# One Trainium2 core, a fused four-layer model: Mamba's front with dt's bias as a matmul row and the residual added by TensorE

## What is computed

```python
def mamba_block(x, Wi, cw, cb, Wx, Wdt, bdt, Alog, Dp, Wo):
    xz = x @ Wi.T
    xs, z = jnp.split(xz, 2, axis=-1)
    u = silu(causal_conv(xs, cw) + cb)
    xdbl = u @ Wx.T
    dt, Bc, Cc = jnp.split(xdbl, [8, 8 + 16], axis=-1)
    dt = jax.nn.softplus(dt @ Wdt.T + bdt)
    A = -jnp.exp(Alog)
    # h = exp(dt A) h + dt B u ;  y = C h
    y = scan(...) + u * Dp
    y = y * jax.nn.silu(z)
    return y @ Wo.T
for i in range(4):
    x = mamba_block(layer_norm(x, ln_w[i], ln_b[i]), ...) + x
```

## Time and profile before

| | us |
|---|---|
| median of 3 runs | 1874.89 (1874.24 to 1879.85) |
| the profiled execution, its own time | 1869.66 |
| its span, first to last instruction | 1867.8 |
| first scan-group instruction to last (L1049) | 110.3 to 1641.6 |
| mean granted TensorE clock over the span | 0.876 of full speed |

### The profile page before, as it was taken

How to read it: one execution, slowest core, us unless ns; L and a number is a source line. 1 busy time by engine, 2 the same in 40 slices (tenths; PEclk the granted TensorE clock), 3 DMA queues, 4 the chain that set the end, 5 groups by cost and what they waited for, 6 DMA issues and landing times.

```text
span 1867.8 us, 28242 instructions
## 1 busy us (share of the span) xinstructions
PE 1482.4 (79%) x9417; PEld 1056.2 (57%) x9417; DVE 1481.1 (79%) x2326; ACT 1339.2 (72%) x2730; POOL 1325.9 (71%) x1767
## 2 busy tenths in 40 slices
PE   6677766666899988567878999778889986889975
PEld 2443433334677666434455777556667664667854
DVE  6588898899999899978987978887988998721254
ACT  4476656666998787767687878788887886654453
POOL 3158678777788789887766867799978897830046
PEclk7676776787999999787788999989999998989997
DMA  5033222433544334220334444332545433212300
GB/s 192 1 75 73 63 66 69 109 82 96 134 119 116 120 108 108 69 59 23 91 102 108 130 126 138 86 107 56 132 137 132 132 96 69 66 43 74 124 6 6
DMA packets 84591, 170.15 MB, mean 91 GB/s; under 512 B 9440, under 2 KB 14944, under 8 KB 84064
## 3 DMA queue, kind: packets, MB, share of 16 engines
q1 hardware_dynamic: 84448, 168.37, 32.9%
HBM read 99.12 MB, written 2.10 MB: 54 GB/s over the span
## 4 chain that ended last, share of the span: by engine, by line
PE 23%; DVE 14%; ACT 9%; POOL 7%; issue 3%; DMA 2%; SPq 0%; DVEq 0%; POOLq 0%; ACTq 0%
DVE m L1049 5%; DVE dtuB L1041 3%; POOL m L1060 3%; PE ps L1467 3%; ACT m L1025 3%; PE ps L1475 2%; PE ps L1314 2%; PE ps L1758 2%; PE ps L1182 2%; PE ps L1080 2%; PE ps L964 2%; POOL o L1660 1%; PE ps L1325 1%; POOL o L1655 1%; ACT L347 1%
## 5 line engine op out<-in xcount | busy, mean ns | idle before, releaser
L1060 POOL TENSOR_TENSOR m<-m 128x256 f32<-128x256 f32 x1024 | 906.7, 920 | 92.5 <-DVE m L1049 84.9
L1049 DVE TENSOR_TENSOR_SCAN m<-m,dtuB 128x1024 f32<-128x1024 f32 x256 | 584.4, 2283 | 32.8 <-PE ps L1080 9.6
L1025 ACT ACTIVATE m<-m,Aneg 128x255 f32<-128x255 f32 x1024 | 429.8, 497 | 24.3 <-DMA m<-m 17.0
L1041 DVE TENSOR_TENSOR dtuB<-m 128x1024 f32<-128x1024 f32 x256 | 347.5, 1357 | 14.0 <-DMA m<-spread 5.2
L1467 PE MATMUL ps<-o 128*128 128x256 f32 x512 | 149.0, 402 | 18.9 <-DVE X L1411 7.1
L1080 PE MATMUL ps<-m,w_const 128*32 128x256 f32 x2048 | 151.5, 426 | 10.2 <-POOL m L1060 10.2
L1434 ACT ACTIVATE o<-ps,w_mo 128x256 f32<-128x256 f32 x256 | 113.4, 470 | 60.1 <-PE ps L1467 58.6
L364 POOL TENSOR_TENSOR o<-o,mhalf 128x2 f32<-128x2 f32 x64 | 19.4, 304 | 170.2 <-DVE o L358 170.2
L1182 PE MATMUL ps<-o 128*128 128x256 f32 x512 | 125.8, 395 | 13.2 <-ACT o L1151 8.2
L964 PE MATMUL ps<-m,wc 128*128 128x256 f32 x512 | 134.4, 421 | 2.0 <-ACT m L385 2.0
L1475 PE MATMUL ps<-o 128*128 128x128 f32 x1024 | 128.8, 279 | 5.5 <-ACT o L1434 4.8
(11 more groups left out here) (251 smaller groups left out, 2909.7 us busy)
## 6 DMA issues: line engine op xcount, KB each, us to landing
m<-m SPq DMA_DIRECT2D x256, 256.0 KB, 4.8
m<-spread SPq DMA_DIRECT2D x64, 512.0 KB, 5.4
o<-in_mox SPq DMA_DIRECT2D x128, 256.0 KB, 3.1
o<-in_l1x SPq DMA_DIRECT2D x88, 256.0 KB, 3.1
w_mb<-in_mb SPq DMA_DIRECT2D x1, 2288.0 KB, 11.8
m<-in_cwr SPq DMA_DIRECT2D x1, 2048.0 KB, 15.6
w_l3f<-in_l3f SPq DMA_DIRECT2D x1, 1536.0 KB, 17.6
X<-in_x SPq DMA_DIRECT2D x4, 256.0 KB, 6.6
```

The lines of the kernel that those rows point to most:

```text
L1025: op = e.activation(dA[at % NA][:, j, 1:CH], R[q][:, h * CH + 1:h * CH + CH], ACT.Exp, scale=Aneg[:, l, 4 * g + j:4 * g + j + 1])
L1041: e.tensor_tensor(dtuB[:, :, :], bc(R[q][:, (2 + h) * CH:(3 + h) * CH].unsqueeze(1), 4, CH), Br[k % 2], ALU.mult).then_inc(S.dve, n.tick(f ...
L1049: e.tensor_tensor_scan(flat(G[at % NG]), flat(dA[at % NA]), flat(dtuB[:, :, :]), 0.0, ALU.mult, ALU.add).then_inc(S.dve, n.tick(f"s{g}"))
L1060: op = e.tensor_tensor(part, part, Cr[k % 2][:, j:j + 1, :], ALU.mult)
```

## The change

It does five things in the front, and the table of turns is new.

1. The bias of dt becomes a 41st row. W_x gets a zero column (41 outputs), the activation that copies them adds a per-partition value that is 1 in row 40 and 0 elsewhere, and W_dt gets the bias as its row 40. The constant "bdt" (2 columns) goes, "one" (1 column) comes.
2. The two Identity activations with the bias go. Abs reads the bank straight away; Ln writes the tile dtu instead of the bank; VectorE's last step reads dt from the bank and the logarithm from dtu.
3. TensorE adds the residual: before the wait for y, two matmuls of the identity with hs open the accumulation in the bank, and the output projection adds to them. VectorE's add is gone.
4. The norm's statistics and the normalization read the bank for l over 0. TensorE's first transpose then waits for both halves, since it overwrites the bank. For the last block X is added from the bank.
5. ScalarE copies the bank into hs for l over 0, after the statistics, in a turn of its own ahead of the normalization.

Turns of ORDER: on TensorE f goes from 192 to 224, on VectorE from 136 to 112, on ScalarE from 200 to 224; all other totals, and all of SyncE (577) and GpSimd (594), are as before. The a and b turns that stand ahead of a given s turn differ by -13 to +15 on TensorE (of 1056), -10 to +5 on VectorE (of 600), -7 to +7 on ScalarE (of 960), -6 to +2 on GpSimd and -4 to +3 on SyncE. After the last s turn, 182, 104, 174, 54 and 58 of them are left, in both tables.

```diff
-MB, NMB = cols([("win", 512), ("wx", 2, 40), ("wdt", 256), ("wout", 2, 128),
-                ("cb", 2), ("bdt", 2), ("alog", 8, 4), ("dp", 2), ("lnw", 1), ("lnb", 1)])
+MB, NMB = cols([("win", 512), ("wx", 2, 41), ("wdt", 256), ("wout", 2, 128),
+                ("cb", 2), ("one", 1), ("alog", 8, 4), ("dp", 2), ("lnw", 1), ("lnb", 1)])
...
 class Front, dve:
                     e.wait_ge(F.pe, n.pe("wo"))
-                    e.tensor_tensor(v.hs, ps2(b), v.hs, ALU.add).then_inc(F.dve, n.tick("hs"))
-                    e.wait_ge(F.dve, n.dve("hs"))
                     if l == NL - 1:
-                        e.tensor_tensor(X2(c), X2(c), v.hs, ALU.add).then_inc(F.dve, n.tick("X"))
+                        e.tensor_tensor(X2(c), X2(c), ps2(b), ALU.add).then_inc(F.dve, n.tick("X"))
                         if k < NU:
                             e.wait_ge(F.dve, n.dve("X"))
-                    yield
+                        yield
...
-                yield from norm_dve(e, n, F, v, v.hs)
+                yield from norm_dve(e, n, F, v, ps2(b) if l else v.hs)
                 e.wait_ge(F.act, n.act("ln"))
-                e.scalar_tensor_tensor(v.dt, v.dt, 0.0, halves_of(b), ALU.max, ALU.add).then_inc(F.dve, n.tick("dt"))
+                e.scalar_tensor_tensor(v.dt, halves_of(b), 0.0, v.dtu, ALU.max, ALU.add).then_inc(F.dve, n.tick("dt"))
...
 class Front, act:
-                norm_act(e, n, F, v, v.hs, v.xn)
+                if l:
+                    e.wait_ge(F.dve, n.dve("mv1"))
+                    e.copy(v.hs, ps2(b)).then_inc(F.act, n.tick("hs"))
+                    yield
+                norm_act(e, n, F, v, ps2(b) if l else v.hs, v.xn)
...
-                e.copy(v.xd[0:40, :], b[0:40, 0:CH]).then_inc(F.act, n.tick("xd"))
+                e.activation(v.xd[0:41, :], b[0:41, 0:CH], ACT.Identity, bias=m("one", l)[0:41, 0:1]).then_inc(F.act, n.tick("xd"))
                 yield
                 e.wait_ge(F.pe, n.pe("wd"))
-                for h in range(2):
-                    e.activation(v.dt[:, h, :], b[:, h * CH:h * CH + CH], ACT.Identity,
-                                 bias=m("bdt", l)[:, h:h + 1]).then_inc(F.act, n.tick(f"v{h}"))
-                e.wait_ge(F.act, n.act("v1"))
-                e.activation(v.dtu, v.dt, ACT.Abs).then_inc(F.act, n.tick("ab"))
+                e.activation(v.dtu, halves_of(b), ACT.Abs).then_inc(F.act, n.tick("ab"))
...
-                e.activation(halves_of(b), v.dtu, ACT.Ln, bias=1.0).then_inc(F.act, n.tick("ln"))
+                e.activation(v.dtu, v.dtu, ACT.Ln, bias=1.0).then_inc(F.act, n.tick("ln"))
...
 class Front, pe:
                     c, l = UNITS[k - 2]
+                    for i in range(2):
+                        e.matmul(b[:, cut(i)], ident, v.hs[:, i, :], start=i == 0, stop=False, skip_group_check=True)
+                    yield
                     e.wait_ge(F.dve, n.dve("y"))
                     for i in range(2):
                         for h in range(2):
-                            op = e.matmul(b[:, cut(i)], v.dtu[:, h, cut(i)], m("wout", l)[:, h, :], start=h == 0, stop=h == 1)
+                            op = e.matmul(b[:, cut(i)], v.dtu[:, h, cut(i)], m("wout", l)[:, h, :], start=False, stop=h == 1,
+                                          skip_group_check=True)
...
+                if l:
+                    e.wait_ge(F.act, n.act("xn1"))
                 turn_pe(e, n, F, b, v.xn)
```

More of the change, by code:

```diff
@@ L209 @@
     "sp":
[L210 to L213, removed]
+        "uf2s4fs4f2sfs7f3s8f3s8f3s8f3s8f3s8f3s8f2sa2s3afs4a6fa2sb3fs4fs3bfb2f2s4b2s4b3a3f3sasas6a3faf2s4a2s2a2b2sa2saf3sb"
@@ new lines @@
+        "a8ua3ua3ba2ba7b2ab2ab7ab2ab2ab5a3bab2a2f2b2abf3abab2aba2ba2ba3sf2afafbfsb7aba4sb2afa2fbsafbfsaf4sabfabf2b2abf3b2"
+        "s2a4b2abasf2a6saba2fbfa2fbf2a2sa3b2asaf2asa2fbfsfa2f2bsbfba2sf2b2f5sb10sb2afb4fs2f2bf2bsf2ab2sbf2saf3a2sf2a2b2a2"
+        "bafafab2afbaf2abasfsa2b3asfbasafa2fabfafabfaba2sbaba5fasbafbababfabfasfbafsfaba4b2a3bfa2b2saba2fba2ba2fbfbsb2fsf"
+        "bfa2b2a2babafabasba3fasa3fba2bfa4bafa2fabfbsb4ab4fab4sb3safa2b2abafb2fsafab2f2b3sb2f2b3sb2fa2bfb3fb3fa5bfsbafa4b"
+        "sbafab5afa2sa3fafbfbfsa4b2ababa4ba5sb2fafb2sba2b2f3af2sb6fb3sb4fba2babasb2f2ba2bafbfasafab2fa3safb2asbfaf3afasb4"
@@ new lines @@
+        "a4b3sf2aba2fbfafa2fbafba2sasba2babafbasa2fb2afbfasafa2fba2bfa3bsba2ba3b2fa2ba3b2abasa3b2abafbab2a2bfa2bafbsbafa2"
+        "fba2bsfab2ab2a3b2ab2sab2fbfb2abfb2fbsb3fbabafab2fb2a2b2abfab2sb2ab2ab7sfa2ba3f2bsf2afa3bab2a2safb2ababa3safa3b2a2"
+        "fsb2fbabfabfa3sfa3b2a3fba2b2asafba2b2afbafsbaf3asb2ab2asaba2f2b3afba2fas2afabafafba2sb2f2basa3fb2fabafa2b2f2bsb3"
+        "fb3ababsa2fba3bfa2fababasfbfbfbsb2ababfa3b6sb2fb2a2b4fsfab2fbsfb2fb2ab5ab5asfb2fb2safabfa3fa2f2bfasa3ba2bab4sa2b"
+        "fa6b2fa2sababa2b2sba5b2ab2aba2safa3baba2b2aba2ba3babababab2ababa6b2a2b2aba2b2aba2b3a2b3ab3a2ba2bababa4ba2ba2baba"
@@ new lines @@
+        "b2abab3ab2ab3ab2ab2abab2ab5ab8ab9a2ba3ba2b5a2b2a4b3ab3abab2a2bab2",
+    "dve":
+        "au2a7u2bu2b7a11ba2fb2fb3a7b5fb2sfs2fs2bsbsbsbsbs2b2s2fs10fafs7a2s2fa3fsfs4as5a2sa2fs2a2sbs2b2asa2fa2ba2fbsbs7bs3"
+        "b3sbfs8fs2fs3as5a2sb2fafa2b2sb3fbsbs8asfs11fsfs9a2f2afasfs3bsfs11b2fa2fbfbsbfs2fabasabab2sbs6fb2s7a2bfsfs2a2sabs"
+        "bas2bs3fs9fsfsas2a2sb2s3as2afsb3abs3fsafs3as8fsabs3fab2fs2asbs3as4ba2fs2abas2abs2afas3fsbsas5bs3a4fabfa2fsas2bs4"
+        "asbsasasb2s2a3ba3ba2fbasb2asa2s3asas2fs2af2a5fab6sb3s2bs2bsfbs4b8abs2fba2b2f2a2fab2s3bsbsb2absb2s4fs3a3fasfs2asa"
+        "s7basasasasfb2sbsbs2fbfs4bs5b4afsab2s5a2bfasfabsb2s7fs7asfa2fs4babsas3bfab2s2bas3as3fsas3fs2as2bs2b2abs2fbas2a2s"
+        "bfsa2fbasa2sbs4bs3faba2sa5bas3bas2ab2afsf2sfb2a6sa2basbsabas2afs2a2s2b3sasasa2bsb2s2fb2f2bs2bfbs2ba2s3b5saba2sba"
+        "b2s2fb2sbs3b2sfsfs2bs2asbs2bs2ba2fs5as2fsfs2as2b2s3as4fafb3fs3bs4as6fs4as2fbfsasb2s3bs4basfs2bs3basfsfsbs5bs5bfa2"
+        "sba2sbs2afsfsa2b2s3bsbsa2sa6fabs2b2a3s4a6ba2babs2afb2a2sbfa2b3s3aba2b2as5b5sb4asbab2s2aba2fafb5a4b2abab3a2bab2ab"
+        "ab3aba2b2a2baba2b5a3b2a6b3a2b3ab3a2ba2b2a5b8aba2b3ab",
@@ new lines @@
+    "act":
+        "a3ua4ua2ua2bua2ba2ba5b2ab3ab4ab2a2b6a3bafabf2abfb2faf2abab2as2bafabsabas2f2sasaf3bfb3sb2sba2sa2sba3s2bf2afbs2bsf4"
+        "as2af2sbafs2b2faf2b2fs2a3sb2a3s2bafasa2sfa2basfasbfasbf2safa4s2bs4a2saf3sfb2af3ab3asfsf2bs2af2bsfsfs2b2sb3sb2s2b3"
+        "s2b2fbf2s2af3bfsbsfs3bf2s3f2a2f2absa2sbafbafba2fs3a2fbfabafbsfs2a2sba2b2s2asaf2a2faba2fbabfsfas2afab2sasasababsa"
+        "s2ab3f2abfs2afbafbfsafab2a2b2abasa2b2sabsasba2faf2sbs2bfbfsfbfaba3basaba2s2a3baf3bas2a3sfa2fba2fsfb4a2s2b2ab2sba"
+        "b3s2ba4bf2b2sfs2afbafsb2f2ab4sbsfafbasfbs2b2sfb2afb2a3safb2asfbabasa4bs2bsasabab2fbsfaba3fsabf2bfbafasab2aba3ba3"
+        "basas2b2ab2abfba2b2fbfs2faf2sfbsbsb2sb8a2fasfbsbsfbs2a2bfbafsa2fafbsabas2a2sabf2bs3fabf3a2fb3s2asa3ba2bsbsabf3ab2"
+        "afafsafs2afasbabs2ab2abas2asbfabfbfs2afafbabfa2bafb2asba3b2saba2sab2a2sabasbasbabfa2fbsabafsa2sbf2ba2fbasafb2a2b"
+        "a2b2s2basab2sbaf2b2fb2asfbab2fbasafb2abfbababab2s3a2b5ab2abasbabfsasf2asbfafbafsfa2basasb2a2bsa2b2a2ba2s2a3bfba3"
+        "bfb2fsbasfabfa2bas2fa3sfab3a2babsbasasbabsafbfabfs2fbafbfsfsb2asab2s2as2b3f2a2bfsa2s2fbafba2f2ab3absaba2f2sbfs3b"
+        "fba2fsbfasbfbsb2absbas2a2sbaf2afa2sbasbf2bafsbfb3sa3sab5s2b3sa2fb2f2b2s2fbfbsfab2fbsb3a2b3sbabs2b3asf2a2bfsbas2a"
+        "fafabaf2sa2ba3babsasbabsb2a2ba4s2a2b2aba3b2a2bsa2bsba4b2sb2a2b2a7babababab2a3bab3ab2a2b2a3babab4a2bab2abababa2b4"
+        "a2ba2ba4b2a4bab2ab3a2b4ab3a2bab4ab3ab4ab4ab4a2babababa2b4a3b3a3bab3ab3a2b3aba2bab2",
@@ L249 @@
     "pool":
[L250 to L253, removed]
+        "ua3ub2ubu2au2afbfu3a2fbfsfs2bsbsfs6fs4asf2s5fsas2bfa2s6fs5fs4asbfbfbs5fs6fs5f2s2fs6bfaf2s5fbs3afs3as2fs5fs2abs3f"
@@ L254 @@
+        "s2bfs5fs3bfs5afas2asasfs6fa4fa2sasa2sasbs2a2ba2fba5bas2asasf2sab4sb5sbfs3b9abf2bs3bsbs4f2sas6fbs2fs5fabs2fs2as3f"
+        "s4afs2bs2bsfs4fs3bsfs2afa2sas4fsa6sa3sabfbfsa4ba5basfsas5b3sbfb5fbsas3b3sbab5fbs2bsfs5afs4fs2bs4f2bs6fs3fsbs4fs3"
+        "fs6afas2afabs2bs2a4faba4bas3a10sb3ab6sbs4b9abs2ba2b3a4b4a10b10a8b4ab2ab4",
 }
@@ L975, in pe @@
                 for h in range(2):
-                    op = e.matmul(b[0:40, 0:CH], m("wx", l)[:, h, :], v.u[:, h, :], start=h == 0, stop=h == 1)
+                    op = e.matmul(b[0:41, 0:CH], m("wx", l)[:, h, :], v.u[:, h, :], start=h == 0, stop=h == 1)
                 op.then_inc(F.pe, n.tick("wx"))
@@ L980, in pe @@
                 for h in range(2):
-                    op = e.matmul(b[:, h * CH:h * CH + CH], m("wdt", l)[0:40, h * 128:h * 128 + 128], v.xd[0:40, :],
+                    op = e.matmul(b[:, h * CH:h * CH + CH], m("wdt", l)[0:41, h * 128:h * 128 + 128], v.xd[0:41, :],
                                   start=True, stop=True)
@@ L1880, in layout @@
         bc = [8 + 16 * w + 4 * j + i for i in range(4) for w in range(2) for j in range(4)]
-        xs = wx[:, bc + list(range(8))]
```

(6 more changed lines are left out.)

35 lines of the change are left out of this document (3 added, 32 removed).

## The result

The changed kernel took 1886.71 us in the median of 7 runs (1875.84 to 1893.06), the kernel before 1875.36 us beside it (1871.78 to 1879.85, 7 runs). The ratio is 1.005 with a 95% interval of 1.003 to 1.007: some 9 us slower, where I forecast 12 us faster and a range that ended at 1878. The profiled execution is the shortest of the seven, 1875.84 us with a span of 1873.7, so it holds little of the loss itself; I read it for what became of the work, and take the sizes from the ratios.

The account below looks back on a forecast made before the run. It took the middle part as a dense list of turns limited by several engines, no single wall. Terms -8.5, -14.5, +1.4, +7.7, +2 and 0 gave -12 us: 1857.7 profiled, 1863 with 5.2 us to the median; range to 1878, down to 1847.

Parts of the forecast that it names:

- Part 6: The new order of turns on all engines: same plan by counts, taken as 0, ends 6 us either way.
- Part 2: Softplus on the dt path: 64 Identity activations removed from ScalarE, claimed to save 14.5 us.
- Parts 1, 3, 4, 5: Front: residual add off VectorE -8.5, hs copy +1.4, residual matmuls +7.7, bank reads and transpose +2; sum +2.6 us.
- TensorE's share: Added identity matmuls counted by TensorE's part of the followed chain, 23 of 58: +7.7 of 19.2 us.
- Rival C: ScalarE's queue at the hs copy: waiting for statistics holds the scan's exponentials; slower by 12 us, 1887 us; chance 0.14.
- Part 4: Residual on TensorE: two identity matmuls a unit, +7.7 us; wrong if their waits for the bank pass 11 us.
- Rival B: Front ready earlier but next scan or fillers hold turns, TensorE's 19.2 us in full: no gain, 1874 us; chance 0.23.

Follow-up runs that it names:

- the hybrids: Changed code with the new order in some stretches of scans and the old order elsewhere, against the kernel before: ratios from 1.0004 to 1.0051.
- softplus part alone: Kernel before with only the bias row and the softplus in three steps, old order, no turn moved: ratio 0.9998 to the kernel before.
- its own run: Changed code in the old order with the two identity matmuls issued three times a unit, against the kernel before: ratio 1.0052.

## Why the prediction was wrong

- **Part 6, the order at 0 with ends of 6 us: this step failed.** It costs 0.8 to 1.0% with the changed code (1.005 and 1.0078 against 0.9974), 14 to 19 us, and 1.3% with the old code. The counts that I took for proof of equality (turns of the other lines ahead of each scan turn) show that both lists keep the same pace. They do not show which turn stands next to which. What the profiles show beside the loss is 10 us more of scan waits, largely given back ahead of y, and 10 to 14 us more in VectorE's instructions, in part outside the scans; neither follows the loss through the hybrids, so by which turns the order costs stays open. The ends of 6 us came from single waits, and no run had put a price on an order; they should have been wider, or the order measured apart.
- **Part 2, softplus at -14.5: failed.** Measured nothing, with -4.7 to +4.1 us as the interval. The activations were on the followed chain, but the chain is, as I read it, one of several of near the same length, and VectorE's turn behind them did not move. The trace before said so in part: the product of a scan waited for the DMA of dt*u only 2.1 us in 4 places, though ScalarE's exponentials waited for that of dt 17.0 us in 17, and 17.7 us in 17 with the softplus part alone. The activation on 41 rows took back 0.1 us a unit as well. I had called it nothing because its columns are the same, though the earlier trace rows had 467 ns for an activation with such a bias and 377 for one of as many columns without. The Trainium skill, "ScalarE: Activation LUTs", section "What ACT_TABLE_LOAD costs", says that each operand that is a pointer to one value per partition adds some 93 ns; 360 to 464 ns, 104 ns more, agrees roughly.
- **Parts 1, 3, 4, 5 together at +2.6**: -2.2 us measured, interval -6.0 to +1.5, so the sum was a little too high, by 1 us or more; which of its terms, no run shows. TensorE's share held in its own run. VectorE's busy time fell by 14 us in the old order. Statistics from the bank cost nothing more: 284 ns against 283, and the estimate of 65 ns for each that I had worked out from the Trainium skill, "VectorE: DVE Perf Modes", section "The TRN2 errata — SBUF-src ops pay a fixed extra latency per instruction", is not what this trace shows.
- **The code as a whole**: -12 forecast, -4.9 measured (0.9974, in the old order).
- **Rival C, ScalarE held at the copy: it did not happen.** The sign came out as its sign, for another reason: ScalarE stood there 3.6 us in one place. The wait that did appear was the one that I had named under Part 4, TensorE's for the bank, at 10.4 us against my bound of 11, and moving it away did not help.
- **Rival B** was right for Part 2.
- VectorE's total, forecast to fall by 13, fell by 2 in the changed kernel. That was the first visible sign that the new order changes the instructions' times; as the hybrids show, it does not measure what the order costs.

## What to carry to other kernels

When a change brings new code and a new hand-written or planned order, price and test them apart: map the old order onto the new code by naming its turns. Here the code was worth -0.26% and the order +0.9%, and the two together looked like a failed idea. A pace that is equal by counts is no evidence for an order. Waits at chosen instructions and the busy time of one engine show that two orders differ, but here neither gave the size of the loss; only the time of the two orders with the same code did. In this dense list a shorter step on one engine gained nothing while the turns behind it on the other engines stayed where they were, and extra work on TensorE, 80% busy, cost a third to under a half of its length even though nothing waited for it.

## What the runs showed of the hardware that was not expected

- The time of single executions of one kernel goes with their mean granted TensorE clock. Over 35 executions of the kernel before the clock lay between 0.865 and 0.889 and the time between 1863.8 and 1885.7 us: a clock lower by 0.001 went with 0.8 us more (0.4 to 0.7 in the four other sets of executions of that kernel). The changed kernel had 0.875 in the mean and 1885.0 us in its first 7 executions and 0.870 and 1885.1 us in the 12 later ones, the same code in the old order 0.881, 0.878 and 0.880 with 1870.1, 1869.8 and 1868.6. Laid to one clock by the common slope (0.71 us for 0.001), 8 to 13 of the 15 to 17 us stay. Whether the lower clock is a cause of the rest or follows from longer gaps on TensorE is open.
- One profile is not enough to place a loss of this size. Two profiles of the same kernel, the changed code in the old order, differ by 6.7 us between the 16th and the 17th y alone (844.0 to 904.0 us, and 839.3 to 892.6).
- A VectorE instruction of 214 ns took 2386 ns beside a long one of GpSimd, and in the other order the same GpSimd instruction stretched its neighbour on VectorE from 1.32 to 3.37 us.
